# Graph network on one core: in the similarity stage the last of 64 gathered columns is fetched by SP, one DMA per row

## The reference

```python
Wh = h @ W + b
Wr, Wc = Wh[row], Wh[col]                 # row, col: the two ends of every edge
sim = sum(Wr * Wc) / max(|Wr| * |Wc|, EPS)
base = adj_v * softplus(...) * (row != col)
prop_pos = segment_sum((base * relu(sim))[:, None] * Wc, row)
prop_neg = segment_sum((base * -relu(-sim))[:, None] * Wc, row)
out = scale * (coeff[0] * prop_pos + coeff[1] * prop_neg + coeff[2] * Wh)
```

## Time and profile before

| | us |
|---|---|
| median of 3 runs | 17267.54 |
| lowest, highest | 17266.72, 17267.86 |
| profiled execution | 17287.82 |
| its span, first to last instruction | 17286.1 |
| similarity stage in it | about 12348 to 14550 |
| POOL busy, whole span | 12216.5 (71%) |
| DVE busy, whole span | 11671.8 (68%) |

### The profile page before, as it was taken

The page is one execution under the profiler, slowest core; times in us unless marked ns, Lnnn a source line. Parts: engine busy times, 40 slices in busy tenths (PEclk is TensorE's granted clock), DMA queues, the critical chain, the costliest instruction groups (busy, mean ns, idle before and its releaser), DMA issues. The chain is left out here.

```text
span 17286.1 us, 115917 instructions
## 1 busy us (share of the span) xinstructions
PE 4026.1 (23%) x22754; PEld 3079.1 (18%) x22754; DVE 11671.8 (68%) x33588; ACT 2959.7 (17%) x3914; POOL 12216.5 (71%) x12294
## 2 busy tenths in 40 slices
PE   2333357676201111123333222222100001000000
PEld 2222256666100000011111212211100000000000
DVE  6777787777663433444444699998555555799998
ACT  1111112222001111123333122222000000111111
POOL 5777747777417777677776777776777776777774
PEclk6555578888655555555555555555555555555555
DMA  2222222222462222222222233333222222344442
GB/s 91 57 63 57 63 75 78 78 78 83 124 181 54 57 63 57 61 57 69 65 70 61 86 119 117 117 116 104 61 77 79 75 75 70 124 142 139 139 142 99
DMA packets 761406, 1522.92 MB, mean 88 GB/s; under 512 B 477594, under 2 KB 478127, under 8 KB 709476
## 3 DMA queue, kind: packets, MB, share of 16 engines
q1 hardware_dynamic: 366688, 1032.87, 16.6%
q0 software_dynamic: 392880, 471.96, 12.4%
q10 hardware_dynamic: 1348, 12.78, 0.2%
HBM read 718.52 MB, written 804.22 MB: 88 GB/s over the span
## 5 line engine op out<-in xcount | busy, mean ns | idle before, releaser
L883 POOL DMA_INDIRECT rows<-tab,idx x8320 | 8340.5, 1002 | 2687.5 <-issue 2544.4
L1190 DVE TENSOR_TENSOR_SCAN rows<-held,last,rows 128x64 f32<-128x64 f32 (+1 forms) x4992 | 1214.9, 326 | 1582.1 <-DMA rows<-tab,idx 1311.2
L530 POOL DMA_INDIRECT moved_rows<-recs,sidx x1664 | 1672.9, 1005 | 606.0 <-issue 506.8
L883 POOL DMA_INDIRECT rows<-sums,idx x1664 | 1573.1, 945 | 511.8 <-issue 506.9
L1012 DVE TENSOR_REDUCE held<-SQ 128x16 f32<-128x1024 f32 x208 | 254.8, 1225 | 1237.1 <-ACT SQ L983 876.5
L952 PE MATMUL dist_ps<-dist_w,a3T 65*128 65x512 f32 x416 | 392.7, 1099 | 2588.9 <-ACT a3T L976 2503.4
L1485 DVE TENSOR_TENSOR_SCAN H<-logits,H,neg_d 128x52 f32<-128x52 f32 x4096 | 904.5, 301 | 50.1 <-ACT logits L1434 32.5
L1515 DVE TENSOR_TENSOR_SCAN DN<-XB,last,VB 128x52 f32<-128x52 f32 x4096 | 910.7, 300 | 0.0
L1515 DVE TENSOR_TENSOR_SCAN DN<-XB,last,PB 128x52 f32<-128x52 f32 x4096 | 908.0, 302 | 2.3
L1939 DVE TENSOR_TENSOR tmp<-own,rows 128x4096 f32<-128x4096 f32 x26 | 115.1, 4426 | 935.3 <-DMA rows<-tab,idx 935.3
L1442 ACT ACTIVATE PB<-XB 128x3328 f32<-128x3328 f32 x64 | 190.5, 2977 | 3188.2 <-DVE XB L1492 3188.2
(11 more groups left out here) (398 smaller groups left out, 16473.2 us busy)
## 6 DMA issues: line engine op xcount, KB each, us to landing
sums<-DN SPq DMA_DIRECT2D x64, 3328.0 KB, 11.2
rows<-tab,idx POOLq DMA_INDIRECT x8320
sums<-rows SPq DMA_DIRECT2D x52, 2048.0 KB
sums_s<-rows SPq DMA_DIRECT2D x52, 2048.0 KB
maxes<-H SPq DMA_DIRECT2D x64, 1664.0 KB
rows<-moved_rows SPq DMA_DIRECT2D x26, 2176.0 KB
spread<-zeros SPq DMA_DIRECT2D x52, 1040.0 KB
own<-spread SPq DMA_DIRECT2D x26, 2080.0 KB
```

The lines of the kernel that those rows point to most:

```text
L530: pool.indirect_dma_start(moved_rows if fill else rec, bass.IndirectOffsetOnAxis(ap=idx[b][:, j:j + 1], axis=0), recs[b][:, j, :], None).t ...
L883: pool.indirect_dma_start(rows[b][:, j, :], None, table, bass.IndirectOffsetOnAxis(ap=idx[b][:, j:j + 1], axis=0)).then_inc(rows_in[b], 16)
L1190: dve.tensor_tensor_scan(rows[b][:, :, f], k, rows[b][:, :, f], last[:, f:f + 1], ALU.mult, ALU.add).then_inc(scanned, 1)
```

## The change

POOL gathers 63 of the 64 columns of each chunk in this stage; its last gather adds 32 to the semaphore in place of 16, so that the count of a chunk stays the same. SP loads the numbers of the last two columns as one row of 256 numbers on one partition (`far`). In each step it loads eight of them at a time into registers, uses the four that belong to the last column, and issues for each a DMA of one row of `tab65` into `rows`: 32 loads and 128 such DMAs per chunk, half of them before the store and half after it. The store in the step of chunk c is now that of chunk c-2 instead of c-1; the last two are stored at the end. DVE waits for the 128 row fetches as well. The other stages that call `gathers` keep all their gathers.

```diff
-    def gathers(pool, table, idx, rows, idx_in, rows_in, free, go, w, n):
+    def gathers(pool, table, idx, rows, idx_in, rows_in, free, go, w, n, own=None):
...
-            for j in range(w):
-                pool.indirect_dma_start(rows[b][:, j, :], None, table,
-                                        bass.IndirectOffsetOnAxis(ap=idx[b][:, j:j + 1], axis=0)).then_inc(rows_in[b], 16)
+            own_n = own or w
+            for j in range(own_n):
+                pool.indirect_dma_start(rows[b][:, j, :], None, table, bass.IndirectOffsetOnAxis(ap=idx[b][:, j:j + 1], axis=0)
+                                        ).then_inc(rows_in[b], 16 if j + 1 < own_n else 16 * (w - own_n + 1))
...
+            far = [alloc(c, f"far{b}", [1, 2 * P], I32) for b in range(2)]
...
                     sp.dma_start(idx[b][:, :], cols(sdst, i * 2 + b)).then_inc(idx_in[b], 16)
+                    sp.dma_start(far[b][:, :].rearrange("a (p t) -> a p t", t=2),
+                                 cols(sdst, i * 2 + b)[:, T - 2:T].unsqueeze(0)).then_inc(far_in[b], 32)
+
+                def fetch_far(i, b, first):
+                    for p in range(first, first + P // 2, 4):
+                        _, v = nc.values_load_multi_w_load_instructions(
+                            far[b][0:1, 2 * p:2 * p + 8], engines=[mybir.EngineType.SP], min_val=0, max_val=NP - 1,
+                            skip_runtime_bounds_check_because="node numbers lie below NP")
+                        for k in range(4):
+                            sp.dma_start(rows[b][p + k:p + k + 1, T - 1, :], tab65[bass.ds(v[2 * k + 1], 1), :]).then_inc(far_rows[b], 16)
...
                         load_indices(*((i, 1) if b == 0 else (i + 1, 0)))
+                    sp.wait_ge(far_in[b], (i + 1) * 32)
                     sp.dma_start(own[b][:, :, :], cols(spread, ch)).then_inc(side_in[b], 16)
                     sp.dma_start(base[b][:, :], cols(sbase, ch)).then_inc(side_in[b], 16)
-                    if not isinstance(i, int) or i or b:
-                        store(ch - 1)
+                    fetch_far(i, b, 0)
+                    if not isinstance(i, int) or i:
+                        store(ch - 2)
+                    fetch_far(i, b, P // 2)
...
                 step(NCH // 2 - 1, 1, last=True)
+                store(NCH - 2)
                 store(NCH - 1)
...
-                gathers(pool, tab65, idx, rows, idx_in, rows_in, lambda e, i, b: e.wait_ge(msg, i * 2 + b - 1), go, T, NCH)
+                gathers(pool, tab65, idx, rows, idx_in, rows_in, lambda e, i, b: e.wait_ge(msg, i * 2 + b - 1), go, T, NCH, T - 1)
...
                     dve.wait_ge(rows_in[b], (i + 1) * 16 * T)
+                    dve.wait_ge(far_rows[b], (i + 1) * 16 * P)
```

More of the change, by code:

```diff
@@ L1861, in similarity_pass @@
         q = lambda n: sem(f"L2_{n}")
-        idx_in, rows_in, side_in = S("idx"), S("rows"), S("side")
+        idx_in, rows_in, side_in, far_in, far_rows = S("idx"), S("rows"), S("side"), S("far_idx"), S("far_rows")
         go, filled, steps, msg, scanned, carried, stored = (q(n) for n in (
```

## The result

| | before | after |
|---|---|---|
| median, us | 17267.13 | 17394.65 |
| lowest, highest | 17265.72, 17267.86 | 17391.62, 17399.22 |
| profiled execution | 17287.82 | 17399.22 |
| period: one first multiply (L1939, now L1956) to the next | 83.15 | 88.0 |

The ratio is 1.0074 (95% interval 1.0057 to 1.0092), +127.5 us. The forecast was +1010 us: right in direction, eight times too large.

What follows compares the result with a forecast made beforehand. POOL's instruction rate was taken to bound the stage; SP's 2.65 + 59.1 + 59.8 = 121.6 us a chunk against POOL's 81.9 gave +1010 us on 17267.5, about 18280 us; range 17240 to 18900 us.

Steps and rivals of the forecast that it cites:

- POOL sets the stage before: POOL's gathers in this stage set the 83.15 us period; one gather fewer per chunk makes it 81.9 us.
- 128 row fetches at 0.462 us, 59.1 us: SP's single-row DMAs with register addresses, per chunk: 59.1 us, ends 46 and 68.
- 32 loads of eight numbers at 1.83 us, 59.8 us: SP's register loads from SBUF per chunk: 0.48 + 7 x 0.193 us each, plus gap; ends 16.6 and 123.5 us.
- the rest: SP's ordinary issues per chunk (idx, own, base, store, far): five at 0.53 us, 2.65 us.
- Change = 26 S - 2151.5: Stage's time change in us, S being SP's step per chunk: +1010 at S = 121.6, break-even at 82.7.
- DVE waits for the store, the loop through store and message does not bind: DVE's chunk c waits for the store of c-1; the loop needs only a period of at least 70.5 us.
- Rival (a): Eight numbers load nearly for the price of one, SP hides under POOL: S = 78.4 us, 17242 us; chance 0.17.
- Rival (b): SP bound, but little: cheap loads with fetches queued behind 2 MB transfers, S = 92.4, 17519 us; chance 0.17.
- the sign that I had named: In SP's queue, long row fetches behind own or the store, 7 us behind each, would show the queueing case.

Runs made afterwards that it cites:

- e6b: Changed kernel with `far` holding only the last column (16 loads of eight, all used) and the store of c-1 back in step c: 17241.26 us, ratio 0.9983.
- e7: Changed kernel, but POOL gathers 62 columns, SP and ACT each fetch two columns for half the partitions, store of c-1 in mid-step: 17209.56 us, ratio 0.9964.
- e3: Changed kernel with 16 loads of eight numbers by a stride of two, all used, instead of 32 loads of eight neighbours: 17541.85 us, ratio 1.0157.
- e8r: Changed kernel with 64 loads of four neighbours a chunk, two fetches each, repeated on a chip with the usual time: 17701.03 us, ratio 1.0248.
- e9r: Changed kernel with 32 loads of four numbers by a stride of two, repeated on a chip with the usual time: 17676.42 us, ratio 1.0234.
- e1: Changed kernel with 128 loads of one number per chunk in place of 32 loads of eight: 18503.55 us, ratio 1.0716.
- e2: Changed kernel with 16 loads of sixteen numbers per chunk in place of 32 loads of eight: 17262.46 us, ratio 0.9997.
- e6: Changed kernel with `far` holding the last column alone, so 16 loads of eight neighbours, all used, per chunk: 17251.33 us, ratio 0.9989.
- e4: Changed kernel without SP's number loads and row fetches, last column zeroed once by DVE and left uncomputed: 17255.11 us, ratio 0.9991.

## Why the forecast was wrong in size

- *POOL sets the stage before, 83.15 us a chunk; a column fewer is 1.25 us.* Right, and shown: e6b has 81.82 and e7 80.66 us.
- *128 row fetches at 0.462 us, 59.1 us.* Close: 57.0. The median DMA is 228 ns, not 272, but the gaps are wider (0.412 us from start to start in the median), and three fetches behind each store take 0.9 to 1.1 us.
- *32 loads of eight numbers at 1.83 us, 59.8 us.* **This step failed.** It took the 193 ns of register work behind the one load of the earlier trace rows as the price of each further number. Measured, a load of eight neighbours takes 0.78 us: 26.2 us, 33.6 less. That is the whole miss of the step: 121.6 - 33.6 = 88.0. That it comes out to the tenth is luck: the fetches' 2.1 us too many and the rest's 2.15 too few (4.8 against 2.65, of which the turn of SP's loop, which the sum left out, is 1.3) cancel.
- *Change = 26 S - 2151.5.* Right. With the measured periods it gives +136 for the changed kernel, +282 for e3, +443 for e8r, +407 for e9r and +1239 for e1; the runs have +127.5, +275, +430, +405 and +1236. Break-even at 82.7 fits, though no run stands close above it: a step of 88.0 lost, one of about 81.5 (e2) came out even, and 74 (e6, e6b) won a little.
- *DVE waits for the store, the loop through store and message does not bind.* Right (998.3 us in 24 waits; SP, not the loop, is never idle). But POOL waited for the message (20 waits), and not for its indices as I had written.
- *Rival (a): 32.5 us won less 7 at the end.* The condition was named rightly (a load of 0.62 us), the prize was not. With a step that fits, the deferred store moves the first multiply to another place against the gathers and costs about 0.6 us a chunk: by the medians 16 to 20 us are won (e4, e6), not 25.
- *Rival (b)*, SP bound but little, came nearest, by its second half: loads of 0.7 to 1.1 us, up to +400. Of its queue there is a little, and the sign that I had named, long fetches behind the store, did appear: three a step and two loads, 41.9 against 39.4 us for the half of a step, so 2.5 us where I had 7. Behind `own` I had another 7, and there is nothing. Whether a full queue makes these fetches long was not tried.

The trace had one load of one number, and 0.48 to 3.82 us was the honest range for eight. Inside it I picked a row for its size and not because it measured the same thing.

## What to carry to other kernels

Work moved to an idle queue is paid in that queue's instruction time: count here about 0.42 us for each small DMA with an address from a register, some 2.5 us more behind a 2 MB store, and the loads beside it, and compare the sum of one step with the period before moving it. Here the step was 6% above the period (88.0 against 83.15), and the sign of the change hung on it. Lay out what registers will read as neighbours and use every number loaded; and give the moved work to two idle queues rather than one (e7, 61 us won, against 30 of e6b).

## What the runs showed of the hardware

SP's load into registers, median us by count of 4-byte numbers from SBUF:

| numbers | 1 | 4 | 8 | 16 |
|---|---|---|---|---|
| neighbours | 0.492 | 0.556 | 0.780 | 1.228 |
| stride of two | | 1.113 | 1.915 | |

Beyond four, a neighbour costs (1.228 - 0.780)/8 = 0.056 us; a number that is no neighbour (1.915 - 1.113)/4 = 0.20 us. The 200 ns per register of the Trainium skill (Runtime: NRT & Kernel Launch, Instruction fetch mechanics), which it gives even for bulk and in a passage on loads from HBM, is what strided loads from SBUF show; for neighbours in SBUF the measurement is a quarter of it. The Trainium skill's floor of about 600 ns (DMA: Bandwidth & Descriptors, Latency and other measured facts) lies above the 0.49 and 0.556 us measured here.

A gather that begins while DVE multiplies two SBUF operands (4.43 us) ends 0.81 to 0.83 us after the multiply, in all 218 such cases of the kernel before, the changed one and the ten runs that have the usual time: 4.09 us when begun 1.14 us into it, 4.78 at 0.46. One that is already running when the multiply begins keeps its 0.94 us. The message's multiply, of the same size but with one operand (`a`) in PSUM, stretches no gather (at most 0.96 us). What holds the gather was not tried.
